# A gated cross-attention and quantised FFN block on one core: level maxima taken as differences of head pairs, five stack rows written instead of three, and a down projection cut by tokens

## What is computed

```python
def _L0_xattn_ref(query, key, value, Wq, bq, Wk, bk, Wv, bv, Wo, bo):   # B=8, S=512, D=256, H=16, DK=16
    q = (query @ Wq + bq).reshape(Bq, Sq, H, DK)
    k = (key @ Wk + bk).reshape(Bq, Sk, H, DK)
    v = (value @ Wv + bv).reshape(Bq, Sk, H, DK)
    scores = jnp.einsum('bqhd,bkhd->hbqk', q, k) / np.sqrt(DK)
    attn = jax.nn.softmax(scores.reshape(H * Bq, Sq, Sk), axis=0).reshape(H, Bq, Sq, Sk)
    out = jnp.einsum('hbqk,bkhd->bqhd', attn, v).reshape(Bq, Sq, H * DK)
    return out @ Wo + bo
...
x = x + jnp.tanh(g_xattn[0]) * _L0_xattn_ref(_layernorm(x), ctx_1024, ctx_1024, ...)
x = x + jnp.tanh(g_ffn[0]) * _L0_ffn_ref(_layernorm(x), ...)
```

## Time and profile before

| | us |
|---|---|
| median of 3 runs | 843.44 |
| lowest, highest of them | 842.04, 1755.95 |
| profiled execution, its own time | 844.21 |
| its span | 842.40 |
| outside the span | 1.81 |

### The profile page before, as it was taken

How to read it: one execution, slowest core, us unless ns; L and a number is a source line. 1 busy time by engine, 2 the same in 40 slices (tenths; PEclk the granted TensorE clock), 3 DMA queues, 4 the chain that set the end, 5 groups by cost and what they waited for, 6 DMA issues and landing times. The chain is left out here.

```text
span 842.4 us, 19948 instructions
## 1 busy us (share of the span) xinstructions
PE 736.4 (87%) x8129; PEld 445.6 (53%) x8151; DVE 756.8 (90%) x739; ACT 678.5 (81%) x1090; POOL 463.9 (55%) x206
## 2 busy tenths in 40 slices
PE   8898897787777769999999999999999999569977
PEld 6564371212122225677766767777677777434344
DVE  4799638999999979999999999999999996949957
ACT  3455449899999979899998999999999933859873
POOL 1343454000000011999999999999999995424500
PEclk9999999999999989999999999999999999979989
DMA  9773589999988637668877786868867794000014
GB/s 295 239 243 113 152 187 243 273 268 283 262 190 202 219 102 242 177 199 281 261 196 210 247 285 210 228 203 282 252 196 214 250 323 140 2 2 1 1 51 150
DMA packets 94987, 165.88 MB, mean 197 GB/s; under 512 B 10160, under 2 KB 37552, under 8 KB 94384
## 3 DMA queue, kind: packets, MB, share of 16 engines
q1 hardware_dynamic: 94896, 164.60, 67.1%
HBM read 142.81 MB, written 42.73 MB: 220 GB/s over the span
## 5 line engine op out<-in xcount | busy, mean ns | idle before, releaser
L1030 POOL TENSOR_TENSOR e<-e,recip 128x2048 f32<-128x2048 f32 (+2 forms) x113 | 361.3, 3236 | 20.9 <-DVE recip L1063 20.8
L980 ACT ACTIVATE e<-psY 128x512 f32<-128x512 f32 x512 | 296.0, 647 | 29.7 <-PE psY L912 24.0
L1050 DVE TENSOR_REDUCE partial<-e 128x128 f32<-128x4096 f32 (+1 forms) x80 | 279.4, 3559 | 6.0 <-ACT e L980 6.0
L912 PE MATMUL psY<-arena 128*128 128x128 bf16 x2048 | 199.8, 220 | 1.3 <-DMA arena<-k_stack 1.2
L912 PEld LDWEIGHTS psY<-arena 128*128 128x128 bf16 x2048 | 148.6, 98 | 74.5 <-issue 25.1
L707 ACT ACTIVATE copies<-ps_max 128x1024 bf16<-128x1024 f32 x189 | 175.5, 1082 | 2.1 <-PE ps_max L686 2.1
L908 PE MATMUL psY<-shift,minus 128*128 128x512 bf16 x396 | 152.2, 384 | 11.2 <-PEq L641 5.5
L723 DVE TENSOR_TENSOR high<-copies,high 128x3072 bf16<-128x3072 bf16 x63 | 109.9, 1745 | 0.4 <-ACT copies L707 0.4
L1019 POOL MEMSET ones_w<- 96x128 bf16 x1 | 0.2, 206 | 174.7 <-POOLq L641 174.7
L718 DVE TENSOR_TENSOR high<-ps_max,high 128x1024 bf16<-128x1024 f32 x63 | 76.4, 1213 | 3.5 <-PE ps_max L686 3.5
L929 PE MATMUL psX<-e,arena 128*32 128x128 f32 x2048 | 75.7, 287 | 3.4 <-issue 1.4
(11 more groups left out here) (171 smaller groups left out, 1000.7 us busy)
## 6 DMA issues: line engine op xcount, KB each, us to landing
arena<-k_stack SPq DMA_DIRECT2D x264, 256.0 KB, 3.4
arena<-q_stack SPq DMA_DIRECT2D x64, 256.0 KB, 4.3
arena<-in_x_dram SPq DMA_DIRECT2D x8, 1024.0 KB, 10.0
k_stack<-parts SPq DMA_DIRECT2D x24, 256.0 KB, 3.1
q_stack<-parts SPq DMA_DIRECT2D x24, 256.0 KB, 3.1
k_stack<-k_stack SPq DMA_DIRECT2D x4, 1536.0 KB, 20.4
q_stack<-q_stack SPq DMA_DIRECT2D x4, 1536.0 KB, 15.3
arena<-in_ctx_dram SPq DMA_DIRECT2D x4, 1024.0 KB, 5.9
```

What stands on the lines that cost most here:

```text
L912: last = nc.tensor.matmul(bank[:, j * P:(j + 1) * P], ks[:, i % KRING, b * P:(b + 1) * P], qs[:, h, b * P:(b + 1) * P], start=False, stop= ...
L980: nc.scalar.activation(e_at(p, half * HB, (half + 1) * HB).rearrange("p q z i -> p z q i"), ps[n % SCORES][:].rearrange("p (z q i) -> p z ...
L1030: nc.gpsimd.tensor_tensor(part, part, by_pairs(recip[:, r % 2, :], share), ALU.mult).then_inc(pool_scaled, 1)
L1050: nc.vector.tensor_reduce(partial[:, :, k, :], e[:, t:t + n].rearrange("p t q z i -> p q i t z"), AX.XY, ALU.add).then_inc(sum_done, 1)
```

## The change

**Stacks.** For chunks 0 to 2 all five needed rows of each group are written from `parts` and three are copied; for the last chunk it stays at three written and five copied. The copies are spread anew over the couples. The wait for the late query copies moves from the end of `maxima` to the first query load of each chunk in `attend`.

**Signs.** Every odd head's K is negated in preparation (in the permuted weights on ACT, and in the bias on DVE, for which ACT now waits).

**Maxima.** `k_mixed` holds the even head in rows 0 to 63 and the negated odd head below (chunks 0 to 2; chunk 3 has zeros below), `k_odd` zeros and the negated odd head. A group is now a couple x one batch, again 64 groups. For chunks 0 to 2 PE computes the difference even - odd (3 matmuls, `ps_x`), ACT takes its relu to bf16 (`gain`), PE computes -odd and subtracts the gain through a negative identity (6 matmuls, `ps_y`), which is minus the larger of both; DVE takes the running minimum from PSUM. For chunk 3 PE computes both heads (2 matmuls, `ps_c`), ACT copies them to bf16, and DVE merges pairs of groups. The shift is now stored negated as `lowest`. For all couples the loads are 14 pieces instead of 12, and couple 0's all stand ahead of the last writes of preparation.

**Attention.** The identity `plus` or `minus` is chosen by the head's sign, exp takes scale 1/4 or -1/4.

**FFN.** Item 42's product moves from POOL to DVE. The row of scales is computed after the first clips, not ahead of the block. Block 0 is rounded, clipped and waited for one token tile (of 4) at a time. The last block is scaled, summed and stored in three parts (2, 1, 1 tiles).

```diff
-K_WRITTEN = (0, 1, 2)
-Q_WRITTEN = (0, 3, 6)
-WRITES = len(K_WRITTEN)
-K_COPIED = (((3, 6), (0, 3)), ((6, 8), (0, 2)))
-Q_COPIED = (((1, 8, 3), (0, 7, 3)), ((2, 6, 3), (0, 4, 3)))
+LAST = 3
+K_WRITTEN = (0, 1, 2, 3, 4)
+Q_WRITTEN = (0, 3, 6, 1, 4)
+K_COPIED = (((5, 8), (2, 5)),)
+Q_COPIED = (((2, 6, 3), (1, 5, 3)), ((7, 8), (6, 7)))
+K_COPIED_LAST = (((3, 6), (0, 3)), ((6, 8), (0, 2)))
+Q_COPIED_LAST = (((1, 8, 3), (0, 7, 3)), ((2, 6, 3), (0, 4, 3)))
...
-    return [(is_q, c, *rows) for rows in (K_COPIED, Q_COPIED)[is_q]]
+    return [(is_q, c, *rows) for rows in ((K_COPIED, Q_COPIED), (K_COPIED_LAST, Q_COPIED_LAST))[c == LAST][is_q]]
...
-COPIES_OF_COUPLE = (2, 2, 3, 2, 3, 2, 2, 0)
+COPIES_OF_COUPLE = (1, 2, 2, 2, 2, 2, 1, 1)
...
+    rows(mixed[0:HALF], k_stack, 2 * p, K_MAX_ROWS)
+    rows(mixed[HALF:P], k_stack, 2 * p + 1, K_MAX_ROWS, NC - 1)
+    for j in range(2):
+        rows(both[j * HALF:(j + 1) * HALF], q_stack, 2 * p + j, Q_MAX_ROWS)
+    rows(odd[HALF:P], k_stack, 2 * p + 1, K_MAX_ROWS)
...
+        def rows_written(u):
+
+            c, g = u // GROUPS, u % GROUPS
+            written = (K_WRITTEN, Q_WRITTEN)[group(c, g)[0]]
+            return written[0:PARTS] if c == LAST else written
...
-                            sp.wait_ge(s["transposed"], TR * (NC - 1))
-                            load_pair(sp, 0, k_stack, q_stack, keep["k_first"], None, keep["q_first"],
-                                      keep["first_loaded"])
+                            sp.wait_ge(s["transposed"], TR * NC)
+                            load_couple(sp, 0, k_stack, q_stack, keep["k_first"], keep["k_odd_first"],
+                                        keep["q_first"], keep["first_loaded"])
...
+                        for at, r in enumerate(rows_written(u)):
                             sp.dma_start(stack[c, h0:h0 + H // DC, r * DK:(r + 1) * DK, :].rearrange("h d x -> d h x"),
-                                         parts[:, u % GB, part, :]).then_inc(stacked[u % GB], 16)
+                                         parts[:, u % GB, at % PARTS, :]).then_inc(stacked[u % GB], 16)
...
+                permute(wk_p, wk_s, "wk_loaded", (1.0, -1.0))
                 for k in range(TR // 2):
                     copy_ctx(k)
                 root_of(0)
                 act.wait_ge(s["b_loaded"], 16 * 2 * DC)
+                act.wait_ge(s["bias_signed"], 1)
...
+                nc.vector.tensor_reduce(sign[:, 0:1], ident[:, 1:P:2], AX.X, ALU.max).then_inc(s["sign_set"], 1)
+                dve.wait_ge(s["sign_set"], 1)
+                nc.vector.tensor_scalar(sign[:, 1:2], sign[:, 0:1], -2.0, 1.0, ALU.mult, ALU.add
+                                        ).then_inc(s["sign_set"], 1)
                 dve.wait_ge(s["b_loaded"], 16 * 2 * DC)
+                dve.wait_ge(s["sign_set"], 2)
+                nc.vector.tensor_scalar(bk_s[:], bk_s[:], sign[:, 1:2], None, ALU.mult).then_inc(s["bias_signed"], 1)
...
-                    sp.wait_ge(keep["k_copied"][c], 16 * len(K_COPIED))
-                    sp.wait_ge(keep["q_copied"][c], 16 * len(Q_COPIED))
-                sp.wait_ge(scored, (H - 2) * UNITS)
+                    sp.wait_ge(keep["k_copied"][c], 16 * len(row_copies(0, c)))
+                sp.wait_ge(keep["q_copied"][0], 16 * len(row_copies(1, 0)))
+                sp.wait_ge(y_scored, MIXED * B * (COUPLES - 1))
...
+                def queries(g):
+                    return q_pair[g // B % 2].rearrange("p c (b q) -> p c b q", q=P)[:, :, g % B, :]
+
+                def keys(tile, g, kc):
+                    return tile[g // B % 2][:, kc, g % B * P:(g % B + 1) * P]
+
+                def differences(g):
+                    p = g // B
+                    if g % B == 0:
+                        pe.wait_ge(loaded[p % 2], 16 * COUPLE_PIECES * (p // 2 + 1))
+                    if g == B:
+                        pe.wait_ge(tiles_zeroed, 2)
+                    for kc in range(MIXED):
+                        if g:
+                            pe.wait_ge(gained, 2 * (g - 1) + (2 if kc == MIXED - 1 else 1))
+                        nc.tensor.matmul(ps_x[:, kc, :], keys(k_mixed, g, kc), queries(g), start=True, stop=True
+                                         ).then_inc(x_scored, 1)
+
+                def plain(g):
+
+                    if g:
+                        pe.wait_ge(c_copied, g)
+                    for j, tile in enumerate((k_mixed, k_odd)):
+                        last_mm = nc.tensor.matmul(ps_c[:, j, :], keys(tile, g, MIXED), queries(g), start=True, stop=True)
+                    last_mm.then_inc(c_scored, 1)
+
+                def smaller(g):
+
+                    for kc in range(MIXED):
+                        if g:
+                            pe.wait_ge(y_merged, 2 * (g - 1) + (1 if kc == 0 else 2))
+                        nc.tensor.matmul(ps_y[:, kc, :], keys(k_odd, g, kc), queries(g), start=True, stop=False)
+                        pe.wait_ge(gained, 2 * g + (2 if kc == MIXED - 1 else 1))
+                        nc.tensor.matmul(ps_y[:, kc, :], minus[:], gain[:, g % RING, kc, :], start=False, stop=True
+                                         ).then_inc(y_scored, 1)
+
+                for g in range(GROUPS):
+                    differences(g)
+                    plain(g)
+                    if g:
+                        smaller(g - 1)
+                smaller(GROUPS - 1)
...
+                for g in range(GROUPS):
+                    if g >= RING:
+                        act.wait_ge(y_scored, MIXED * (g - RING + 1))
+                    for k0, k1 in ((0, MIXED - 1), (MIXED - 1, MIXED)):
+                        act.wait_ge(x_scored, MIXED * g + k1)
+                        nc.scalar.activation(gain[:, g % RING, k0:k1, :], ps_x[:, k0:k1, :], ACT.Relu
+                                             ).then_inc(gained, 1)
+                    act.wait_ge(c_scored, g + 1)
+                    if g % 2 == 0 and g // 2 > RING:
+                        act.wait_ge(c_merged, 2 * (g // 2 - RING))
+                    dst = copies[:, g // 2 % RING, :, g % 2, :] if g >= 2 else last[:, :, g, :]
+                    nc.scalar.activation(dst, ps_c[:], ACT.Copy).then_inc(c_copied, 1)
...
+                def merge(m, j):
+
+                    if j == 0:
+                        dve.wait_ge(c_copied, 2 * m + 2)
+                    if m > 1:
+                        dve.wait_ge(c_merged, 2 * (m - 2) + j + 1)
+                    nc.vector.tensor_tensor(last[:, j], copies[:, m % RING, j], last[:, j], (ALU.max, ALU.min)[j]
+                                            ).then_inc(c_merged, 1)
+
+                for g in range(GROUPS):
+                    for n, (k0, k1) in enumerate(((0, 1), (1, MIXED))):
+                        dve.wait_ge(y_scored, MIXED * g + k1)
+                        if g:
+                            dve.wait_ge(y_merged, 2 * (g - 1) + n + 1)
+                            nc.vector.tensor_tensor(lowest[:, k0:k1, :], ps_y[:, k0:k1, :], lowest[:, k0:k1, :], ALU.min
+                                                    ).then_inc(y_merged, 1)
+                        else:
+                            nc.vector.tensor_copy(lowest[:, k0:k1, :], ps_y[:, k0:k1, :]).then_inc(y_merged, 1)
+                    if g > 2:
+                        merge((g - 1) // 2, (g - 1) % 2)
+                merge(GROUPS // 2 - 1, 1)
+                merges = 2 * (GROUPS // 2 - 1)
+                dve.wait_ge(c_merged, merges)
+                for j, op in enumerate((ALU.max, ALU.min)):
+                    nc.vector.tensor_tensor(folds[:, j, :], last[:, j, 0, :], last[:, j, 1, :], op).then_inc(c_merged, 1)
+                dve.wait_ge(c_merged, merges + 2)
+                nc.vector.scalar_tensor_tensor(out=lowest[:, MIXED, :], in0=folds[:, 0, :], scalar=-1.0, in1=folds[:, 1, :],
+                                               op0=ALU.mult, op1=ALU.min).then_inc(folded, 1)
...
+                    if h == 0:
+                        sp.wait_ge(keep["q_copied"][qc], 16 * len(row_copies(1, qc)))
...
-                        nc.tensor.matmul(bank[:], minus[:], shift_at(qc, kc).to_broadcast([P, HB, P]),
+                        nc.tensor.matmul(bank[:], (plus, minus)[h % 2][:], shift_at(qc, kc).to_broadcast([P, HB, P]),
...
+                                ACT.Exp, scale=(DK ** -0.5, -DK ** -0.5)[half // 2]).then_inc(exped, 1)
...
+                return k % PAIR_ITEMS in POOL_I and k != ITEMS - 2
...
-                    step(nc.vector.tensor_scalar(row[:], wd_row[:], h_scale[:, 1:2], tanh_g[:, 1:2], ALU.mult, ALU.mult))
...
+            ENDS = ((0, 2), (2, 3), (3, 4))
...
+                    for t in range(TB):
+                        nc.scalar.activation(hi[:, 0:IC, tokens(t)], hs[:, 0:IC, tokens(t)], ACT.Copy,
+                                             scale=h_scale[:, 2:3]).then_inc(s["h_rounded"], 1)
+                    for n in range(1, NB):
...
+                    for t in range(TB):
```

(28 more changed lines are left out.)

224 lines of the change are left out of this document (92 added, 132 removed).

## The result

The changed kernel took a median of 828.62 us (4 runs, 826.71 to 830.23) beside 842.76 for the kernel before (one of whose four runs took 1755.95 and is left out of the ratio); the ratio is 0.983 with an interval of 0.981 to 0.986. The profiled execution took 828.47 with a span of 826.70, against 833.6 forecast for it.

The account below looks back on a forecast made before the run. In maxima DVE and ACT were taken as full. Maxima -10.6, end of preparation +3.7 and +0.3, FFN -4.0 sum to -10.6: profiled 844.21 becomes 833.6, median 832.8 us; range 818 to 846.

Parts of the forecast that it names:

- The group's period: Maxima: the loop through PE, ACT and DVE sets 2.49 us a group, bounds 2.38 and 2.80.
- The rival of a group at 2.80: Maxima: handovers between relu, PE and DVE eat the gain, group stays at 2.80, total 844; chance 0.14.
- that of exposed weight loads: Maxima: each of PE's eight waits a group exposes its weight load, PE needs 3.2, total about 870; chance 0.08.
- Relu and copy in turn: Maxima, rival: alternating them makes ACT load tables, 128 loads, +164, total about 1000; chance 0.02.
- The queue in maxima: Maxima: waits for loads behind row copies, 4.5 at couple 3 and 3.0 at couple 4, total 7.5, bounds 0 and 15.
- The clock at the start of maxima: Start of maxima: PE at 1.2 GHz after its longer wait, 1.0 added.
- the queue doesn't matter: Maxima and preparation, rival: no waits for loads, no clock loss, no later start; -22.8, total 820.6; chance 0.20.
- The end of preparation: Preparation's end: 0.875 MiB more loads ahead of the last writes delay it +3.7, bounds 0 and 5; bias and weights +0.3.
- FFN: FFN: item 42 and the down projection's start and end together bring -4.0.
- First tile, row and end: Down projection: earlier start by a smaller first tile -2.3, row of scales off the chain -0.4, shorter end -1.8.
- Item 42's +0.5: FFN, ahead of the last two reductions: item 42 on DVE adds a step of 0.67 less 0.2 free, +0.5.
- Attention: Attention: same work before and after, signs and identities change no count; 0, bounds -2 and 2.

Follow-up runs that it names:

- the three orders: TensorE's matmuls in the changed kernel's order, smaller maxima before plain, or smaller maxima first: 2.47, 2.37, 2.86 us a group; medians 828.62, 825.63, 848.46 us (one run).
- the two traces: Profiles of the unedited changed kernel, one from its first measurement and one from its repeat in five more rounds; medians 828.62 and 829.18 us.
- the kernel with three rows: Changed kernel with three rows of every chunk written and five copied, copies 2, 2, 3, 2, 3, 2, 2, 0 as before the change; 840.37 us.
- copies in attention: Changed kernel with smaller maxima before plain, last writes not awaited, item 42 on GpSimd, and six row copies moved from the maxima's queue into the attention; 832.22 us.
- copies spread: Changed kernel with row copies between the couples' loads dealt 1, 2, 1, 1, 1, 2, 2, 3 instead of 1, 2, 2, 2, 2, 2, 1, 1; 827.42 us.

## Why the prediction was nearly right

**The group's period: right.** 2.49 predicted, 2.47 measured, and the loop it was worked out from is shown by the three orders. That relu costs a copy's time holds (1.02 and 1.03 us). Relu and copy in turn load no tables, as the Trainium skill has it (ScalarE: Activation LUTs, table sets): the trace has one load in the whole stage, ahead of the exp. The rival of a group at 2.80 falls with it, and so does that of exposed weight loads: PE's waits leave 2.47, and 2.37 in another order. The drain was 5.9 against 5.8.

**The queue in maxima: the term that failed.** The mechanism was right: couple 3, with 3 MiB of copies ahead of its loads, waits in five of six traces, and waits 0.4 at most when they are spread. The size was not: 7.5 predicted, 1.6 and 2.2 in the two traces. "The added 0.375 MiB for the negated odd head makes the loads 15.4" and "3.0 for each MiB copied" are together too long by 1.1 to 3.4 a couple, as the kernel with three rows shows; between couple 5's first issue and the end of its 1.5 MiB of copies lie 18.8, where 15.4 + 4.5 is 19.9. An excess of that size, added up over couples that had no slack in the forecast, made two waits of 4.5 and 3.0 out of one of 1.5. Of the 8.2 that maxima gained beyond the forecast, 5.9 are this term (7.5 - 1.6), 1.5 the group's (64 x 0.024) and 0.7 the clock's (next paragraph). The rate of the loads, 157 GB/s, was as before. The figure that the prediction cited from the Trainium skill (DMA: Bandwidth & Descriptors, the table of measured HBM to SBUF loads), 341 GB/s for 1 MB, doesn't carry over to these loads in pieces of 128 to 256 KB.

**The clock at the start of maxima: right in kind, and it scatters.** The forecast had 1.0. The lower clock costs 0.3 up to ACT's first relu (1.03 and 1.05 behind PE's first matmul, where 0.7 was forecast), and in the second trace 1.0 more between groups 1 and 2: 0.3 and 1.3 in two traces of one kernel, both behind a wait of PE of 3 to 4 us.

**The rival "the queue doesn't matter": near in one term, wrong as a cause.** It gave 820.6, 8.0 below the median where the forecast was 4.2 above it. Its term for maxima, -19.1, is near the measured -18.8, but not for its reason: the loads' rate is as before, and the queue is why the preparation writes five rows, for with three the gain is gone (840.4). Its other half, no later start, is wrong by 5.1.

**The end of preparation: right in kind, its size within the scatter.** PE started 5.1 later in one trace and 3.3 in the other, where 4.0 was forecast. What holds it was half named: with the last writes not awaited, PE still waits 2.5 behind ACT's end for couple 0's own loads. The added loads of couple 0 stand ahead of the last writes: with three rows written, SyncE's wait is still 9.7 and PE's start 4.1 behind ACT's end. What I had at nothing, the 24 more writes, shows as well: ACT's last step came at 126.5 and 125.6, against 122.0 with three rows. But with the same instructions it came between 123.9 and 127.1 in six traces, so the share of these writes isn't settled. The early wait for the bias was covered, as predicted.

**FFN: right.** First tile, row and end brought 3.7 of 4.5, shown by undoing them (3.5). The start gave 2.4 (from the reduction of `hmax` to PE's first matmul on data 4.0, before 6.5), the end 2.3, and the 1.0 between them went the other way; what holds PE there no experiment took apart. Item 42's +0.5 is a term of 0.4 in the tail (6.2 against 5.8); the whole stage scattered from 98.6 to 100.9, so its +0.5 in the ledger proves nothing. But the three traces with item 42 on GpSimd again have 98.6 to 99.2 and the nine others of the changed kernel and its variants 99.0 to 100.9, so it may cost more than that; no run changed it alone.

**Attention: +1.3, not explained.** In eleven traces with the new order of signs, copies in attention aside, it took 391.5 to 394.0, against 391.1 in the one of before. In its first 5 us the granted clock was 0.73 before, and 0.60 and 0.55 in the two traces of the changed kernel, by my estimate 0.7 to 0.9 us at full speed; but copies spread had 0.68 there and took 393.7, so this isn't the whole of it, and no experiment took it apart.
